# Loading the FFN weights early and in chunks in a fused attention and FFN kernel on eight cores

## The chip, the cores and the metric

The kernel runs on one Trainium2 chip, on all of its 8 cores. Each core computes its own 2 of the 16 sequences with the same program; nothing is exchanged between cores. The metric is the device time of one execution in microseconds, that of the slowest core.

## What is computed

One layer: windowed attention over channels, residual and layer norm, then a gated FFN with int weights scaled by 1/127, residual and layer norm. Cut to what matters:

```python
# x: (16, 4096, 1024) f32; W_qkv (1024, 3072); W_out (1024, 1024)
# w_gate, w_up: (3072, 1024) int32; w_down: (1024, 3072) int32
def attn(x, W_qkv, b_qkv, W_out, b_out):      # 16 heads of 64, windows of 256, step 128
    qkv = (x @ W_qkv + b_qkv)                  # q, k, v per head
    a = einsum('bhndw,bhnew->bhnde', qw, kw) * 64 ** -0.5
    o = einsum('bhnde,bhnew->bhndw', softmax(a), vw)
    return o.reshape(...)[:, :L] @ W_out + b_out
def ffn(x, w_gate, w_up, w_down):
    gate = einsum('bsd,hd->bsh', x, w_gate / 127)
    up = einsum('bsd,hd->bsh', x, w_up / 127)
    return einsum('bsh,dh->bsd', silu(gate) * up, w_down / 127)
x = layernorm(x + attn(x, ...))
out = layernorm(x + ffn(x, ...))
```

## The kernel before

The program has two phases, each an instruction block of its own, written with one queue of instructions per engine and explicit semaphore waits. SP and POOL issue all DMAs: SP the plain loads, POOL the stores and the loads that cast f32 or int32 to bf16.

**Phase A** is attention. For each of the core's 2 sequences it walks over t = 0 to 17: step t makes q, k and v for one block of 128 rows (three passes of matmuls, L498 and L503, against `wqkv_bf`, which holds all of W_qkv in SBUF: 128 partitions x 8 x 3072 bf16, 48 KB each), the scores of window t-1, and for window t-2 the transposes, the second attention matmul, the copies `attn_out` (L751, ScalarE), the output projection (L697, L702), the residual `y1pre` (L720, VectorE) and the layer norm (L769 to L804, ScalarE). One window's output is 256 rows, handled as two halves k2. Each half needs its rows of x again, in f32, in `xr32`: SP loads them at L685, 512 KB each, two buffers, each load waiting for the residual two halves before. The last qkv pass belongs to t = 16 of the second sequence; the windows 14 and 15 (steps t = 16 and 17) are finished after it. The results go to DRAM twice, as `y1dbg` in f32 (L731, POOL) and, transposed and in bf16, as `y1fm_scr` (L345, POOL). The next window's attention waits for the residual of the one before (L631).

In between, phase A prepares the FFN weights: 56 jobs (24 for gate, 24 for up, 8 for down), each a casting load into `w_in_bf`, a scaling on VectorE (L389), transposes on TensorE (L403), a copy to `wT_stage` (L413) and a store to a scratch tensor in DRAM (L423 and L426: `wgT_scr`, `wuT_scr`, `wdT_scr`). Two jobs run in a step; the last job is left over and runs after the last step. Its stores stand behind the `y1dbg` stores in POOL's queue.

**Phase B** is the FFN. All engines first wait for everything of phase A (`a_end`), since its SBUF tiles lie where those of phase A did. Then SP loads the three transposed weights whole, 6144 KB each, with one DMA each on one semaphore, `wl0` (L921 to L923), and each matmul group of the gate waits for all three (`wload_tok`). The loop runs over 32 groups g of 256 rows. SP's loads for group g are 8 of `y1fm_sb` (64 KB each, L942) and 2 of `y1r32` (512 KB each, L950), two buffers each. In a group, 24 steps hc go over the hidden units, 128 at a time: 8 matmuls for gate (L984, 128x256 results), 8 for up (L993), SiLU on ScalarE (L1071), the product `h_bf` on VectorE (L1014), and, one step behind, 4 matmuls for down (L965, L969). TensorE's order in a step is gate(hc), up(hc), down(hc-1). Then come the residual `y2pre` (L1034) and the second layer norm, whose work is spread over the steps of the next group.

Of the kernel before, what the change touches and what calls it, by code (L numbers as in the profile page):

```python
# [9 lines left out]
BF16 = mybir.dt.bfloat16  # L10
# [50 lines left out]
def build_program(debug=False, seqs=SEQS, l=L):  # L61
# [32 lines left out]
    for s in ["T", "V", "A", "G",  # L94
              "xq0", "xq1", "xq2", "xq3", "xr0", "xr1", "wl0",
              "tx0", "tx1", "tv0", "tv1", "ty0", "ty1", "tw0", "tw1",
              "wc0", "wc1", "wc2", "wc3", "wi0", "pk0", "pk1", "pf0", "pf1", "pw0", "pw1",
              "yf0", "yf1", "yr0", "yr1", "st0", "st1"]:
        b.sem(s)
# [11 lines left out]

    wqkv_bf = SA("wqkv_bf", [128, 8, 3 * D], BF16)
    wout_bf = SA("wout_bf", [128, 8, D], BF16)
# [130 lines left out]
    with nc.Block() as blk:  # L244
# [212 lines left out]
        def prep_trs(n_tr):  # L457
            k = 0
            while wprep_tr[0] < wprep_ld[0] and k < n_tr:
# [4 lines left out]
                k += 1  # L464

        emit_xload(0)
        emit_xload(1)
# [4 lines left out]
        for s in range(SEQSv):  # L472
            for t in range(TB + 1):
# [113 lines left out]
                if have_qkv:  # L587
                    emit_qkv_pass(2)
                    qkv_free[0] = evac_half[((gt, 2), 1)]
                    emit_xtr(gt + 2)  # L590

                if have_qkv:
# [247 lines left out]
        while wprep_tr[0] < len(wprep_jobs):  # L840
# [4 lines left out]
            wprep_tr[0] += 1  # L845
        flush_typf()

        @blk.sync
# [15 lines left out]
    SBB = lambda n, sh, dt, **kw: es_b.enter_context(nc.sbuf_tensor(n, sh, dt, **kw))  # L864
    wgT = SBB("wgT", [128, 24, D], BF16)
    wuT = SBB("wuT", [128, 24, D], BF16)
# [29 lines left out]
    with nc.Block() as blk:  # L896
# [20 lines left out]
        @blk.sync  # L917
        def _(q):
            for tk in a_end:
                b.wait(q, "Q", tk)  # L920
            b.inc(q.dma_start(wgT[:, :, :], wgT_h.ap().transpose([1, 0, 2])), "wl0", 16)  # L921
            b.inc(q.dma_start(wuT[:, :, :], wuT_h.ap().transpose([1, 0, 2])), "wl0", 16)  # L922
            b.inc(q.dma_start(wdT[:, :, :], wdT_h.ap().transpose([1, 0, 2])), "wl0", 16)  # L923
        wload_tok = b.tok("wl0")

        b2bases = {}

        def nb2(g):
            return b2bases[g] + (24 if g == 0 else 40)

        for g in range(NGg):
            s = g // (Lv // 256)
            r0 = 256 * (g % (Lv // 256))
            gsl = g % 2
            b2base = [b.cnt["A"] if g == 0 else nb2(g - 1)]
            b2bases[g] = b2base[0]

# [15 lines left out]
            rload_done[g] = b.tok("yr%d" % gsl)  # L953

            def emit_down(hc, g=g):
                hsl = hc % 2

                @blk.tensor
                def _(t_, g=g, hc=hc, hsl=hsl):
                    b.wait(t_, "T", mul_done[(g, hc)])  # L960
                    if hc == 0:
# [13 lines left out]
            for hc in range(24):  # L975
# [3 lines left out]
                def _(t_, g=g, gsl=gsl, hc=hc, hsl=hsl):  # L979
                    b.wait(t_, "T", wload_tok)  # L980
                    b.wait(t_, "T", dload_done[g])
# [7 lines left out]
                @blk.tensor  # L989
                def _(t_, g=g, gsl=gsl, hc=hc, hsl=hsl):  # L990
                    b.wait(t_, "T", mul_done.get((g, hc - 2) if hc >= 2 else (g - 1, 22 + hc)))
                    for dc in range(8):
                        b.inc(t_.matmul(up_ps[hsl], wuT[:, hc, 128 * dc:128 * (dc + 1)],  # L993
                                        y1fm_sb[:, gsl, dc, :],
                                        start=(dc == 0), stop=(dc == 7)), "T", 1)
# [27 lines left out]
                if hc >= 1:  # L1023
                    emit_down(hc - 1)
            emit_down(23)

# [11 lines left out]
            for rs in range(2):  # L1038
                apply2_done[(g, rs)] = ("A", nb2(g) + (8 + 8 * rs if g == NGg - 1 else 26 + 3 * rs))

            def emit_vln2(rs, g=g, s=s, r0=r0):
# [136 lines left out]
```

How the kernel before makes its waits and increments, by code:

```python
    def inc(self, instr, name, by=1):  # L40
        instr.then_inc(self.sems[name], by)
        self.cnt[name] += by
        return (name, self.cnt[name])
# [4 lines left out]
    def wait(self, eng, engkey, tok):  # L48
        if tok is None:
            return
        name, val = tok
        if val <= 0:
            return
        key = (engkey, name)
        if self.waited.get(key, 0) >= val:
            return
        self.waited[key] = val
        eng.wait_ge(self.sems[name], val)
# [1085 lines left out]
        @blk.gpsimd  # L1144
        def _(g_):
            g_.wait_ge(b.sems["st0"], b.cnt["st0"])
            g_.wait_ge(b.sems["st1"], b.cnt["st1"])
```

## Time and profile before

| what | us |
|---|---|
| median of 3 executions | 3465.74 (3463.91 to 3727.74) |
| the profiled execution | 3468.05 |
| its span on the slowest core (core 5) | 3466.5 |
| spans of the eight cores | 3447.6 to 3466.5 |
| TensorE busy | 2970.2 (86%) |
| last matmul of phase A to first of phase B | 82.4 |

A page of the profile is one execution on the slowest core. Its parts are the busy time of each engine, the span in slices, the DMA queues, the chain of work that ended last, the costliest groups of instructions, and the DMA issues with their size and the time from issue to landing. PE is TensorE, PEld its weight loads, DVE VectorE, ACT ScalarE, POOL GpSimd, SP SyncE; L12 is a line of the kernel. The granted clock is the share of full speed that TensorE's clock was given in a stretch. Behind the page the trace can be asked for any stretch: the timeline of instructions, the waits by who waited for whom, and tables of busy time by window.

### The profile page before, as it was taken

How to read it: one execution, taken by the hardware profiler on the slowest of the kernel's cores; microseconds unless marked ns; L12 is line 12 of the kernel's file. 1: busy time of each engine (PE TensorE's matmuls, PEld its weight loads, DVE VectorE, ACT ScalarE, POOL GpSimd, SP SyncE). 2: the span in 40 equal slices, each digit the busy share in tenths (PEclk: the TensorE clock that was granted, in tenths of full speed). 3: DMA queues.
4: the chain of work that ended last, by engine and by line, in shares of the span. 5: the costliest groups of instructions: out<-in, count | busy, mean ns of one | idle time of the engine just before them, and what ended most of it. 6: DMA issues, size and time to landing. Idle time of an engine off the chain costs nothing.

```text
span 3466.5 us, 61589 instructions; the slowest of 8 cores (3447.6 to 3466.5 us)
## 1 busy us (share of the span) xinstructions
PE 2970.2 (86%) x23572; PEld 1996.9 (58%) x23572; DVE 935.4 (27%) x1750; ACT 1248.6 (36%) x2721; POOL 184.1 (5%) x324
## 2 busy tenths in 40 slices
PE   1877787778766772599999999999999999999997
PEld 0344444344433331377777777777777777777775
DVE  0434444344433331022122122221222222212211
ACT  0245454524443343034334233343332333433323
POOL 1001111101111100000000000000000000000000
PEclk9999999899998896799999999999999999999998
DMA  7134434333443324511111011111110111111100
GB/s 128 49 88 125 110 107 119 101 86 98 122 128 103 104 80 155 169 39 42 44 50 44 32 50 44 45 36 44 50 44 31 50 44 50 36 39 50 44 32 25
DMA packets 108737, 245.73 MB, mean 71 GB/s; under 512 B 11424, under 2 KB 44192, under 8 KB 108448
## 3 DMA queue, kind: packets, MB, share of 16 engines
q0 software_dynamic: 43744, 138.96, 14.1%
q1 hardware_dynamic: 64704, 102.82, 8.9%
q8 instruction: 193, 3.16, 0.4%
q14 instruction: 96, 0.79, 0.1%
HBM read 175.16 MB, written 102.76 MB: 80 GB/s over the span
## 4 chain that ended last, share of the span: by engine, by line
PE 58%; SPq 2%; ACT 0%; DMA 0%; DVE 0%; issue 0%; POOL 0%; ACTq 0%; DVEq 0%; POOLq 0%
PE psum_qkv L984 19%; PE psum_O L965 10%; PE psum_S L993 10%; PE psum_TR L993 10%; PE psum_O L969 10%; SPq L942 1%; SPq L923 1%; SPq L922 0%; DMA y1fm_sb<-y1fm_scr 0%; DVE y2pre L1034 0%; ACT y L1141 0%; ACT y2sq L1124 0%; ACT y2sq L1121 0%; ACT L1121 0%; DVE h_bf L1014 0%
## 5 line engine op out<-in xcount | busy, mean ns | idle before, releaser
L984 PE MATMUL psum_qkv<-y1fm_sb,wgT 128*128 128x256 bf16 x6144 | 797.9, 273 | 82.4 <-DMA y1fm_sb<-y1fm_scr 82.4
L984 PEld LDWEIGHTS psum_qkv<-y1fm_sb,wgT 128*128 128x128 bf16 x6144 | 601.8, 98 | 309.8 <-issue 82.7
L1071 ACT ACTIVATE sg_bf<-psum_qkv 128x256 bf16<-128x256 f32 x768 | 293.7, 382 | 1181.6 <-PE psum_S L993 672.6
L965 PE MATMUL psum_O<-wdT,h_bf 128*128 128x512 bf16 x1536 | 581.9, 379 | 0.6 <-DVE h_bf L1014 0.6
L969 PE MATMUL psum_O<-wdT,h_bf 128*128 128x512 bf16 x1536 | 582.0, 379 | 0.0
L993 PE MATMUL psum_S<-y1fm_sb,wuT 128*128 128x256 bf16 x3072 | 399.0, 273 | 0.0
L993 PE MATMUL psum_TR<-y1fm_sb,wuT 128*128 128x256 bf16 x3072 | 398.6, 273 | 0.0
L1014 DVE TENSOR_TENSOR h_bf<-psum_S,sg_bf 128x256 bf16<-128x256 f32 x384 | 163.1, 425 | 815.6 <-PE psum_O L965 717.4
L1014 DVE TENSOR_TENSOR h_bf<-psum_TR,sg_bf 128x256 bf16<-128x256 f32 x384 | 163.1, 425 | 795.0 <-PE psum_O L965 675.7
L498 PE MATMUL psum_qkv<-wqkv_bf,x_fm 128*128 128x512 bf16 x816 | 315.3, 386 | 48.8 <-DVE q_tm L531 44.3
L993 PEld LDWEIGHTS psum_S<-y1fm_sb,wuT 128*128 128x128 bf16 x3072 | 301.0, 98 | 35.2
L993 PEld LDWEIGHTS psum_TR<-y1fm_sb,wuT 128*128 128x128 bf16 x3072 | 300.9, 98 | 35.1
L503 PE MATMUL psum_qkv<-wqkv_bf,x_fm 128*128 128x512 bf16 x816 | 314.5, 385 | 7.6 <-DVE q_tm L534 7.1
L697 PE MATMUL psum_O<-wout_bf,attn_out 128*128 128x512 bf16 x512 | 228.1, 446 | 8.4 <-ACT attn_out L751 8.4
L702 PE MATMUL psum_O<-wout_bf,attn_out 128*128 128x512 bf16 x512 | 224.3, 438 | 0.4 <-ACT attn_out L751 0.4
L965 PEld LDWEIGHTS psum_O<-wdT,h_bf 128*128 128x128 bf16 x1536 | 150.0, 98 | 119.9 <-issue 21.2
L969 PEld LDWEIGHTS psum_O<-wdT,h_bf 128*128 128x128 bf16 x1536 | 150.0, 98 | 98.6
L769 ACT ACTIVATE y1sq<-y1pre 128x1024 f32<-128x1024 f32 x64 | 67.6, 1057 | 300.3 <-DVE y1pre L720 297.1
L498 PEld LDWEIGHTS psum_qkv<-wqkv_bf,x_fm 128*128 128x128 bf16 x816 | 80.7, 99 | 154.8 <-issue 72.9
L1071 ACT ACT_TABLE_LOAD x63 | 80.8, 1283 | 193.2 <-PE psum_S L993 98.5
L751 ACT ACT_TABLE_LOAD x32 | 41.1, 1283 | 298.7 <-PE psum_S L311 160.7
L1058 POOL DMA_DIRECT2D out<-y x64 | 34.1, 533 | 2074.0 <-ACT y L1105 1860.1
(145 smaller groups left out, 2441.9 us busy)
## 6 DMA issues: line engine op xcount, KB each, us to landing
xr<-x SPq DMA_DIRECT2D x64, 512.0 KB, 3.2
y1dbg<-y_f POOLq DMA_DIRECT2D x64, 512.0 KB, 3.0
y1r<-y1dbg SPq DMA_DIRECT2D x64, 512.0 KB, 4.2
out<-y POOLq DMA_DIRECT2D x64, 512.0 KB, 2.9
y1fm_scr<-y1fm_stage POOLq DMA_DIRECT2D x8, 2048.0 KB, 7.2
y1fm_sb<-y1fm_scr SPq DMA_DIRECT2D x256, 64.0 KB, 2.0
xt_bf<-x POOLq DMA_DIRECT2D x34, 256.0 KB, 8.1
wqkv_bf<-wqkv POOLq DMA_DIRECT2D x8, 768.0 KB, 27.9
```

What stands on the lines that cost most here:

```text
L498: b.inc(t_.matmul(psum_qkv[:, 0:512], lhsT, wqkv_bf[:, c, 1024 * p:1024 * p + 512], start=(c == 0), stop=False), "T", 1)
L503: b.inc(t_.matmul(psum_qkv[:, 512:1024], lhsT, wqkv_bf[:, c, 1024 * p + 512:1024 * (p + 1)], start=(c == 0), stop=False), "T", 1)
L697: b.inc(t_.matmul(pj[:, 0:512], lhsT, wout_bf[:, c, 0:512], start=(c == 0), stop=False, skip_group_check=True), "T", 1)
L702: b.inc(t_.matmul(pj[:, 512:1024], lhsT, wout_bf[:, c, 512:1024], start=(c == 0), stop=False, skip_group_check=True), "T", 1)
L751: b.inc(a.activation(attn_out[:, hp, rb:rb + 256] .rearrange("p (d c) -> p d c", c=4), psum_O[:, base:base + 256] .rearrange("p (c d) -> p ...
L769: b.inc(a.activation(y1sq[:, :], y1pre[:, rsl, :], AF.Identity, accum_out=sums[:, rsl, :]), "A", 1)
L965: b.inc(t_.matmul(down_ps[:, 1024 * rs:1024 * rs + 512], lhsT, wdT[:, hc, 0:512], start=(hc == 0), stop=(hc == 23), skip_group_check=True) ...
L969: b.inc(t_.matmul(down_ps[:, 1024 * rs + 512:1024 * (rs + 1)], lhsT, wdT[:, hc, 512:1024], start=(hc == 0), stop=(hc == 23), skip_group_ch ...
L984: b.inc(t_.matmul(gate_ps[hsl], wgT[:, hc, 128 * dc:128 * (dc + 1)], y1fm_sb[:, gsl, dc, :], start=(dc == 0), stop=(dc == 7)), "T", 1)
L993: b.inc(t_.matmul(up_ps[hsl], wuT[:, hc, 128 * dc:128 * (dc + 1)], y1fm_sb[:, gsl, dc, :], start=(dc == 0), stop=(dc == 7)), "T", 1)
L1014: b.inc(v.tensor_tensor(h_bf[:, hsl, :], up_ps[hsl], sg_bf[:, hsl, :], ALU.mult), "V", 1)
L1071: b.inc(a.activation(sg_bf[:, hsl, :], gate_ps[hsl], AF.Silu), "A", 1)
```

## The change

- `wqkv_bf` is placed at the other end of SBUF (`side="right"`) in a stack of its own, which is closed after the last qkv pass has been emitted; `wgT`, of the same size, is then opened in its place.
- `emit_wg_stream`, called in the last qkv step of the last sequence (t = 16), right after the last qkv pass, puts into SP's queue: a wait for the last qkv matmul, waits for the stores of the prepared weights emitted so far, and the load of `wgT`, 6144 KB in one DMA, with its own semaphore `wg0`. It stands ahead of the `xr32` loads of window 14 in SP's queue.
- In phase B the three big loads are gone. `emit_gloads` holds the loads of a group; those of g = 0 and 1 stand first in SP's queue, those of g + 2 follow after group g.
- `wuT` and `wdT` are loaded in 24 chunks each of 128 x 1024 bf16 (256 KB). Up front come wu 0, wd 0, wu 1, wd 1, wd 2; in group 0, after step hc, chunk hc + 2 of each. wu(hc) waits for up(hc - 2), wd(hc) for down(hc - 3), with semaphores taken in turn (two for wu, three for wd).
- TensorE waits for `wg_tok` before a gate group, for `wu_tok[hc]` before up and `wd_tok[hc]` before down.

```diff
@@ -92,7 +92,8 @@
     es_outer = contextlib.ExitStack()
     b = Bld(nc, es_outer)
     for s in ["T", "V", "A", "G",
-              "xq0", "xq1", "xq2", "xq3", "xr0", "xr1", "wl0",
+              "xq0", "xq1", "xq2", "xq3", "xr0", "xr1",
+              "wl0", "wl1", "wl2", "wl3", "wl4", "wg0",
               "tx0", "tx1", "tv0", "tv1", "ty0", "ty1", "tw0", "tw1",
               "wc0", "wc1", "wc2", "wc3", "wi0", "pk0", "pk1", "pf0", "pf1", "pw0", "pw1",
               "yf0", "yf1", "yr0", "yr1", "st0", "st1"]:
@@ -109,7 +110,10 @@
     es_a = contextlib.ExitStack()
     SA = lambda n, sh, dt, **kw: es_a.enter_context(nc.sbuf_tensor(n, sh, dt, **kw))
 
-    wqkv_bf = SA("wqkv_bf", [128, 8, 3 * D], BF16)
+    es_qkv = contextlib.ExitStack()
+    wqkv_bf = es_qkv.enter_context(
+        nc.sbuf_tensor("wqkv_bf", [128, 8, 3 * D], BF16, side="right"))
+    wgT_holder = [None]
     wout_bf = SA("wout_bf", [128, 8, D], BF16)
     bq_rep = SA("bq_rep", [128, 3 * D], BF16)
     bo_rep = SA("bo_rep", [128, D], BF16)
@@ -463,6 +467,20 @@
                 wprep_tr[0] += 1
                 k += 1
 
+        def emit_wg_stream(gt_last):
+            es_qkv.close()
+            wgT_holder[0] = es_outer.enter_context(
+                nc.sbuf_tensor("wgT", [128, 24, D], BF16, side="right"))
+            pw_fin = [b.tok("pw0"), b.tok("pw1")]
+
+            @blk.sync
+            def _(q, gt_last=gt_last, pw_fin=pw_fin):
+                b.wait(q, "Q", qkv_mm_done[(gt_last, 2)])
+                for tk in pw_fin:
+                    b.wait(q, "Q", tk)
+                b.inc(q.dma_start(wgT_holder[0][:, :, :],
+                                  wgT_h.ap().transpose([1, 0, 2])), "wg0", 16)
+
         emit_xload(0)
         emit_xload(1)
         emit_xload(2)
@@ -588,6 +606,9 @@
                     emit_qkv_pass(2)
                     qkv_free[0] = evac_half[((gt, 2), 1)]
                     emit_xtr(gt + 2)
+
+                if s == SEQSv - 1 and t == TB - 1 and wprep_tr[0] >= 24:
+                    emit_wg_stream(gt)
 
                 if have_qkv:
                     vbk, vqtok = claim_tr()
@@ -844,6 +865,9 @@
             prep_transpose(wprep_tr[0])
             wprep_tr[0] += 1
         flush_typf()
+        if wgT_holder[0] is None:
+            emit_wg_stream(SEQSv * TB - 1)
+        wg_tok = b.tok("wg0")
 
         @blk.sync
         def _(q):
@@ -862,7 +886,7 @@
 
     es_b = contextlib.ExitStack()
     SBB = lambda n, sh, dt, **kw: es_b.enter_context(nc.sbuf_tensor(n, sh, dt, **kw))
-    wgT = SBB("wgT", [128, 24, D], BF16)
+    wgT = wgT_holder[0]
     wuT = SBB("wuT", [128, 24, D], BF16)
     wdT = SBB("wdT", [128, 24, D], BF16)
     y1fm_sb = SBB("y1fm_sb", [128, 2, 8, 256], BF16)
@@ -918,22 +942,29 @@
         def _(q):
             for tk in a_end:
                 b.wait(q, "Q", tk)
-            b.inc(q.dma_start(wgT[:, :, :], wgT_h.ap().transpose([1, 0, 2])), "wl0", 16)
-            b.inc(q.dma_start(wuT[:, :, :], wuT_h.ap().transpose([1, 0, 2])), "wl0", 16)
-            b.inc(q.dma_start(wdT[:, :, :], wdT_h.ap().transpose([1, 0, 2])), "wl0", 16)
-        wload_tok = b.tok("wl0")
-
-        b2bases = {}
-
-        def nb2(g):
-            return b2bases[g] + (24 if g == 0 else 40)
-
-        for g in range(NGg):
+
+        wu_tok, wd_tok = {}, {}
+
+        def emit_wu_chunk(hc):
+            @blk.sync
+            def _(q, hc=hc):
+                b.wait(q, "Q", up_done.get((0, hc - 2)))
+                b.inc(q.dma_start(wuT[:, hc, :], wuT_h.ap()[hc]),
+                      "wl%d" % (hc % 2), 16)
+            wu_tok[hc] = b.tok("wl%d" % (hc % 2))
+
+        def emit_wd_chunk(hc):
+            @blk.sync
+            def _(q, hc=hc):
+                b.wait(q, "Q", down_done.get((0, hc - 3)))
+                b.inc(q.dma_start(wdT[:, hc, :], wdT_h.ap()[hc]),
+                      "wl%d" % (2 + hc % 3), 16)
+            wd_tok[hc] = b.tok("wl%d" % (2 + hc % 3))
+
+        def emit_gloads(g):
             s = g // (Lv // 256)
             r0 = 256 * (g % (Lv // 256))
             gsl = g % 2
-            b2base = [b.cnt["A"] if g == 0 else nb2(g - 1)]
-            b2bases[g] = b2base[0]
 
             @blk.sync
             def _(q, g=g, s=s, r0=r0, gsl=gsl):
@@ -952,11 +983,32 @@
                           "yr%d" % gsl, 16)
             rload_done[g] = b.tok("yr%d" % gsl)
 
+        emit_gloads(0)
+        if NGg > 1:
+            emit_gloads(1)
+        for c0 in (0, 1):
+            emit_wu_chunk(c0)
+            emit_wd_chunk(c0)
+        emit_wd_chunk(2)
+
+        b2bases = {}
+
+        def nb2(g):
+            return b2bases[g] + (24 if g == 0 else 40)
+
+        for g in range(NGg):
+            s = g // (Lv // 256)
+            r0 = 256 * (g % (Lv // 256))
+            gsl = g % 2
+            b2base = [b.cnt["A"] if g == 0 else nb2(g - 1)]
+            b2bases[g] = b2base[0]
+
             def emit_down(hc, g=g):
                 hsl = hc % 2
 
                 @blk.tensor
                 def _(t_, g=g, hc=hc, hsl=hsl):
+                    b.wait(t_, "T", wd_tok[hc])
                     b.wait(t_, "T", mul_done[(g, hc)])
                     if hc == 0:
                         b.wait(t_, "T", resid2_done.get((g - 1, 1)))
@@ -977,7 +1029,7 @@
 
                 @blk.tensor
                 def _(t_, g=g, gsl=gsl, hc=hc, hsl=hsl):
-                    b.wait(t_, "T", wload_tok)
+                    b.wait(t_, "T", wg_tok)
                     b.wait(t_, "T", dload_done[g])
                     b.wait(t_, "T", silu_done.get((g, hc - 2) if hc >= 2 else (g - 1, 22 + hc)))
                     for dc in range(8):
@@ -988,6 +1040,7 @@
 
                 @blk.tensor
                 def _(t_, g=g, gsl=gsl, hc=hc, hsl=hsl):
+                    b.wait(t_, "T", wu_tok[hc])
                     b.wait(t_, "T", mul_done.get((g, hc - 2) if hc >= 2 else (g - 1, 22 + hc)))
                     for dc in range(8):
                         b.inc(t_.matmul(up_ps[hsl], wuT[:, hc, 128 * dc:128 * (dc + 1)],
@@ -1022,6 +1075,10 @@
                     pending_vln2[0] = None
                 if hc >= 1:
                     emit_down(hc - 1)
+                if g == 0 and hc + 2 <= 23:
+                    emit_wu_chunk(hc + 2)
+                    if hc >= 1:
+                        emit_wd_chunk(hc + 2)
             emit_down(23)
 
             for rs in range(2):
@@ -1037,6 +1094,9 @@
 
             for rs in range(2):
                 apply2_done[(g, rs)] = ("A", nb2(g) + (8 + 8 * rs if g == NGg - 1 else 26 + 3 * rs))
+
+            if g + 2 < NGg:
+                emit_gloads(g + 2)
 
             def emit_vln2(rs, g=g, s=s, r0=r0):
                 rstd2_done = ("A", nb2(g) + (7 + 8 * rs if g == NGg - 1 else 22 + rs))
```

## Rows read from the trace of the kernel before

**Rows 1.** The page's first lines, and the waits of all engines: waited for, times, longest.

```profile
span 3466.5 us, 61589 instructions; the slowest of 8 cores (3447.6 to 3466.5 us)
PE 2970.2 (86%) x23572; PEld 1996.9 (58%) x23572; DVE 935.4 (27%) x1750; ACT 1248.6 (36%) x2721; POOL 184.1 (5%) x324
...
PE psum_qkv L984 <- DMA y1fm_sb<-y1fm_scr: 82.4, 1, 82.4
```

**Rows 2.** Timeline (start, duration, engine, line) of TensorE, 1338 to 1460 us.

```profile
1343.28 1.01 PE L311 MATMUL psum_qkv<-ident_sb,y_bf 128*128 128x128 bf16 x8 [10.93 <-DVE wT_stage L413]
...
1426.74 1.86 PE L984 MATMUL psum_qkv<-y1fm_sb,wgT 128*128 128x256 bf16 x8 [82.45 <-DMA y1fm_sb<-y1fm_scr]
...
1428.39 1.91 PE L993 MATMUL psum_S<-y1fm_sb,wuT 128*128 128x256 bf16 x8
...
1430.10 1.91 PE L984 MATMUL psum_qkv<-y1fm_sb,wgT 128*128 128x256 bf16 x8
...
1433.99 1.04 PE L984 MATMUL psum_qkv<-y1fm_sb,wgT 128*128 128x256 bf16 x8
...
1434.86 1.04 PE L993 MATMUL psum_S<-y1fm_sb,wuT 128*128 128x256 bf16 x8
...
1436.60 1.04 PE L984 MATMUL psum_qkv<-y1fm_sb,wgT 128*128 128x256 bf16 x8
```

**Rows 3.** Timeline of SP, 1359 to 1430 us; the duration is that of the issues.

```profile
1359.32 0.38 SPq L921 DMA_DIRECT2D wgT<-wgT_scr  x1
1359.75 13.65 SPq L922 DMA_DIRECT2D wuT<-wuT_scr  x1
1373.45 20.88 SPq L923 DMA_DIRECT2D wdT<-wdT_scr  x1
1394.37 26.77 SPq L942 DMA_DIRECT2D y1fm_sb<-y1fm_scr  x8
...
1422.12 4.12 SPq L942 DMA_DIRECT2D y1fm_sb<-y1fm_scr  x8
```

**Rows 4.** Timeline of DVE and POOL at the end of phase A.

```profile
1298.40 1.23 DVE L720 TENSOR_TENSOR y1pre<-psum_O,xr 128x1024 f32<-128x1024 f32 x1 [7.49 <-PE psum_O L697]
...
1338.38 0.53 POOL L731 DMA_DIRECT2D y1dbg<-y_f  x1 [6.95 <-ACT y_f L801]
...
1349.51 0.89 POOL L345 DMA_DIRECT2D y1fm_scr<-y1fm_stage  x1 [0.74 <-issue]
```

**Rows 5.** Table by windows: length, busy us, then granted clock, DMA share, GB/s.

```profile
1290.00:1310.00 20.00, 11.78 (x60) 5.49 (x60) 6.52 (x10) 13.01 (x30) 0.53 (x1) 0.82 0.22 79
...
1375.00:1395.00 20.00, 0.00 (x0) 0.00 (x0) 0.00 (x0) 0.00 (x0) 0.00 (x0) 0.50 0.98 303
...
1427.00:1447.00 20.00, 20.00 (x136) 14.46 (x135) 2.97 (x7) 3.97 (x8) 0.00 (x0) 0.86 0.18 64
```

**Rows 6.** DMA issues over the span: count, KB each, median us to landing.

```profile
xr<-x SPq DMA_DIRECT2D x64, 512.0 KB, 3.2
...
y1fm_sb<-y1fm_scr SPq DMA_DIRECT2D x256, 64.0 KB, 2.0
...
wgT<-wgT_scr SPq DMA_DIRECT2D x1, 6144.0 KB, 25.0
```

**Rows 7.** L942 in two windows: landing of the first and second set of 8.

```profile
L942 SPq DMA_DIRECT2D y1fm_sb<-y1fm_scr x8: 477/600/19652, 1394.4 to 1420.5; - x8
...
DMA to landing us min/median/max: 4.2/6.7/26.7
...
DMA to landing us min/median/max: 2.8/3.7/5.0
```

**Rows 8.** Timeline of SP and TensorE; L423's stores between 1000 and 1300 us.

```profile
1265.75 0.33 SPq L685 DMA_DIRECT2D xr<-x  x1
...
1282.85 0.38 PE L510 MATMUL psum_qkv<-bq_rep,ones 128*128 128x512 bf16 x1
...
L423 POOL DMA_DIRECT2D wdT_scr<-wT_stage x21: 885/885/927, 1032.0 to 1198.9; - x21
```

## The prediction

> **What bounds the kernel now.** I read the page first. TensorE is busy 86% of a span of 3466.5 us, and most of the list of waits is engines waiting for TensorE; the one wait of TensorE itself that stands out is 82.4 us, once, on the loads of y1fm_sb [rows 1]. Then I read the timeline of that spot. TensorE ends its last transposes of phase A at 1344.3 (1343.28 + 1.01) and starts the first gate group of phase B at 1426.74 [rows 2]. SP issues its first DMA of phase B at 1359.32 [rows 3]; before that it waits for the last store of y1fm_scr, which POOL issued at 1349.51 [rows 4]. So the hole has two parts: 15.0 us of storing (1359.3 - 1344.3) and 67.4 us in which 3 x 6144 KB of weights and then y1fm_sb come in (1426.7 - 1359.3). The table by windows shows that second part as DMA at 0.98 of its time and 303 GB/s with no matmul [rows 5]. The rest of phase B is TensorE back to back: a step over one hidden chunk (8 gate, 8 up, 4 down matmuls) is 1436.60 - 1433.99 = 2.61 us, its gate group 0.87 us [rows 2], and there the change alters nothing.
>
> **The sum goes against** the profiled execution's own 3468.05 us; the median of the runs is 3465.74, 2.3 us less.
>
> **Phase B, what goes.** TensorE no longer waits for the three big loads. In SP's queue now come the group loads of g=0 (8 of y1fm_sb, 2 of y1r32), those of g=1, and then wu0, wd0, wu1, wd1, wd2. Call T0 the moment of SP's first DMA (1359.3 before). An issue takes 0.43 us and 0.04 us to the next: the second set of 8 took 4.12 us in all with one long one in it [rows 3], and I give the y1r32 loads the same. The 8 loads of g=0 are out at T0 + 3.8; they land 2.0 us after issue when nothing is ahead [rows 6], so gate 0 starts near T0 + 5.5. That is not yet the gain: up 0 needs wu0, and wu0 is the 21st DMA. 20 issues x 0.47 = 9.4 us. What it then takes to land: the trace has no 256 KB load here, the nearest rows are 2.0 us for 64 KB and 3.2 for 512 KB on an idle queue [rows 6], which would be about 2.5, and 2.8 to 5.0, median 3.7, for the second set of y1fm_sb, which had 1 MB of y1r32 ahead [rows 7]. wu0 stands in the second position (3 MB issued ahead of it in 9.4 us, about what 303 GB/s [rows 5] carries), so I take 3.7 and keep 2.5 and 5.0. Up 0 then starts at T0 + 9.4 + 3.7 + 0.1 = T0 + 13.2. wd0, wu1, wd1 and wd2 follow 0.47 us apart and are wanted 3 us later or more at the clock of that moment (gate 1 alone takes 1.7, below).
>
> **Phase B, the stream.** Chunk hc+2 of wu is issued once up(hc) is done and wanted at up(hc+2). Between lie down(hc-1), gate(hc+1), up(hc+1), down(hc) and gate(hc+2), five blocks of 0.87 us: 4.35 us of cover. It needs about 0.1 for the semaphores and 2.5 to land (2.0 and 3.2 as bounds). So 1 to 2 us are to spare and it costs nothing; wd has one step more. Both are issued on SP, where only each other's waits are in the way: wd(hc+2) waits for down(hc-1), 0.87 us after up(hc). The load is 0.52 MB in 2.61 us = 201 GB/s, under the 303 of [rows 5]. If a chunk landed in 5.0 us, the worst of the loaded rows [rows 7], each of 22 steps would lose 0.7 us, 15 in all: the upper bound. SP's own next work, the loads of g=2, comes behind the last chunk, and is wanted only a group (over 60 us) later as before. [...]
>
> **Phase A, what is added.** The load of wgT (6144 KB) goes into SP's queue ahead of the xr32 loads of window 14 of the second sequence. Before, the first of those was issued at 1265.75 [rows 8], right after the y1pre of the window before, and was wanted by the y1pre at 1298.40 [rows 4]. Now SP first waits for the last qkv matmul, which starts at 1282.85 and ends at 1283.2 (the weight stores it also waits for are long out: the 21 of wdT_scr before 1300 begin by 1198.9, and the last job's three are emitted behind) [rows 8], and issues wgT at 1283.3. The next DMA on the queue is not through until half of the big one is gone: wuT behind wgT took 13.65 us to issue, wdT behind wuT 20.88, and y1fm_sb's first 19.65 of the 26.77 that its eight took [rows 3]. So xr32's issue ends at 1283.8 + 13.7 = 1297.5, just when it is wanted. Its data stand behind the rest of wgT, which lands 25.0 us after its issue [rows 6], at 1308.4, and 0.5 MB more at 303 GB/s is 1.7 us: 1310.1, and y1pre at 1310.2 instead of 1298.4. That is a delay of d = 11.8 us.
>
> Would it be absorbed? Layer norm of both halves goes straight into the attn_out copies, proj and LN of window 15; ACT and TensorE alternate to y_f, y1dbg at 1338.38, the wdT_scr store queued behind it on POOL, and y1fm_scr at 1349.51 [rows 4]. Each waits for the one ahead, so all d reaches the end of phase A, and T0 becomes 1371.1. The bounds of d: the first y1fm_sb read as landed 26.7 us after issue start [rows 7], that is 1421.1, or 7.1 after its issue ended; by that xr32 lands at 1304.6 and d = 6.2. Above: a slower landing under the other cores' load, 13. The first y1fm_sb shares its semaphore with seven others, so I trust the full landing more and take 11.8.
> The Trainium skill, page "DMA: Bandwidth & Descriptors", section "Queues, rings and completion order", says that each DMA engine takes the descriptors of a ring in order and that all rows of one issuing engine share those rings. By it xr32 can't overtake wgT and the sum is the one with 11.8; by the early reading of the row it would be 5.6 us better. The trace leaves it open.
>
> **The clock.** After the hole TensorE's granted clock is at its lower level (1.2 GHz): the up group takes 1.71 us start to start, and 0.87 at full clock (2.4 GHz) a few us later [rows 2]; the window from 1427 to 1447 has 0.86 [rows 5]. The same ramp is paid after the change, but gate 0 is cut off from up 0 by 5 us of waiting, so perhaps one group more runs slow: 1.0 us (0 to 3).
>
> **Sum.** Up 0 starts at 1371.1 + 13.2 = 1384.3 instead of 1428.39 [rows 2]: -44.1. The clock: +1.0. Stream: 0. That is 3468.05 - 43.1 = 3425.0 for the profiled execution, and less 2.3 it is 3423 for the median.
>
> **Rivals.**
> *A, the xr32 loads lose nothing* (d = 0: wgT is spread so that the later DMA gets through, or xr32 lands in time). For it speaks only the early landing of [rows 7]. The gain is 55, time 3411.
> *B, the stream stalls lightly.* Landings of 4.6 to 5.5 us; for it speak the 5.0 of [rows 7], against it that those had other loads ahead. 0.3 to 1.2 us x 22 = 7 to 26 us: 3430 to 3449.
> *C, slower than before: the stream stalls and TensorE stays at half clock through g=0.* In the attention tail, where TensorE works in bursts between waits, the granted clock is 0.82 [rows 5]. If each of 24 steps ran at half clock, each would cost 2.61 more, less some 2 us of ramp already paid: +60, and 3423 + 60 = 3483, 17 slower than before. At half clock the cover is 8.7 us too, so the stall would have to be long: it decides from about 6.4 us per landing (4.35 + 44/22), which no row of a 64 or 512 KB load on SP beside normal traffic shows [rows 6].
> The Trainium skill, page "TensorE: Matmul & The Clock Gate", section "HAM oscillation — how this bites in real kernels", describes just this: a loop whose tiles each wait for a DMA runs with the array held at half clock. It speaks against the change only if there is a wait in each step; by it the time is C's.
> *D, more in the attention tail.* The hole of 12 us there drops the clock once more, or xr32's second load comes late too: 5 to 10 us, 3428 to 3433. Against it: the tail was already mostly slow or waiting.
>
> **Chances.** Forecast 0.70 (alone 3413 to 3432), A 0.08, B 0.12, C 0.04, D 0.06. The range 3406 to 3440 holds the forecast, A, D and the lower half of B. Two per cent, about what a measurement can tell from no change, is 69.3 us. More than the 67.4 us that lie between T0 and the first matmul can't be had, and the g=0 loads must still come; so faster by over 2% gets 0.02, slower by over 2% (C with heavy stalls besides) 0.02, within 2% 0.96.
>
> **What would show it.** In the profile after: (1) TensorE's longest wait on y1fm_sb falls from 82.4 to some 20 us, with a second one of about 5 us on wuT; (2) the xr32 load of window 14 shows an issue of some 13 us and y1pre at about 1310; (3) SP's first DMA of phase B near 1371; (4) the first gate near 1377, up 0 near 1384; (5) the 24 steps of g=0 in about 65 us at a clock of 0.9 or more. The forecast is wrong if y1pre stays at 1298 (A), if up matmuls in g=0 wait for wuT in every step (B), or with a clock below 0.8 there (C).

## The result and the profile after

The changed kernel is faster by 1.2%: the ratio to the kernel before is 0.9883, 95% interval 0.9869 to 0.9897, which makes 3425 us of 3466. That is clear of noise, and under two per cent. Executions in which a die ran at a lowered clock are left out of it. The forecast was 3423 with a range of 3406 to 3440. The profiled execution took 3430.02 us against 3468.05, 38 us less, where 43.1 less had been forecast for it.

The page's first lines, and the waits of TensorE from 1200 to 1460 us on the slowest core, which is core 6 here (waited for, in total, times, longest):

```profile
span 3428.5 us, 61374 instructions; the slowest of 8 cores (3411.3 to 3428.5 us)
PE 2937.0 (86%) x23218; PEld 1995.8 (58%) x23572; DVE 935.6 (27%) x1750; ACT 1247.8 (36%) x2721; POOL 184.1 (5%) x324
...
PE psum_qkv L1036 <- DMA y1fm_sb<-y1fm_scr: 22.1, 1, 22.1
PE psum_qkv L315 <- ACT y_bf L825: 17.0, 1, 17.0
PE psum_qkv L315 <- DVE wT_stage L417: 10.9, 1, 10.9
...
PE psum_S L1046 <- DMA wuT<-wuT_scr: 7.9, 1, 7.9
```

The wait of 82.4 us [rows 1] has become 22.1, and two smaller ones stand beside it: 7.9 us on the first chunk of wuT, and in the attention tail a wait for y_bf, which was 5.3 us before and is 17.0. The timelines of SP, DVE and TensorE show where each comes from (some lines of each):

```profile
1285.60 0.39 SPq L481 DMA_DIRECT2D wgT<-wgT_scr  x1
1286.08 29.16 SPq L706 DMA_DIRECT2D xr<-x  x4
1373.02 3.81 SPq L973 DMA_DIRECT2D y1fm_sb<-y1fm_scr  x8
1376.88 0.92 SPq L981 DMA_DIRECT2D y1r<-y1dbg  x2
1377.83 4.79 SPq L973 DMA_DIRECT2D y1fm_sb<-y1fm_scr  x8
1382.67 0.91 SPq L981 DMA_DIRECT2D y1r<-y1dbg  x2
1383.62 0.43 SPq L952 DMA_DIRECT2D wuT<-wuT_scr  x1
```

```profile
1312.29 2.55 DVE L741 TENSOR_TENSOR y1pre<-psum_O,xr 128x1024 f32<-128x1024 f32 x2 [19.18 <-DMA xr<-x]
```

```profile
1381.19 1.87 PE L1036 MATMUL psum_qkv<-y1fm_sb,wgT 128*128 128x256 bf16 x8 [22.11 <-DMA y1fm_sb<-y1fm_scr]
1391.00 1.86 PE L1046 MATMUL psum_S<-y1fm_sb,wuT 128*128 128x256 bf16 x8 [7.94 <-DMA wuT<-wuT_scr]
1392.66 1.67 PE L1036 MATMUL psum_qkv<-y1fm_sb,wgT 128*128 128x256 bf16 x8
1394.17 1.04 PE L1046 MATMUL psum_TR<-y1fm_sb,wuT 128*128 128x256 bf16 x8
```

y1pre now waits 19.18 us for xr32, where it used to wait 7.49 for the projection [rows 4]. Phase B's first DMA goes out at 1373.02 instead of 1359.32, and up 0 starts at 1391.00 instead of 1428.39 [rows 2, 3]. After that the stream costs nothing to see: a step of group 0 takes 2.61 us, as before. In the table by windows (core 6; the last three columns are granted clock, DMA share and GB/s), TensorE is busy throughout while 201 GB/s come in:

```profile
1400.00:1420.00 20.00, 19.84 (x151) 14.86 (x153) 3.40 (x8) 2.77 (x8) 0.00 (x0) 1.00 0.62 201
```

The cores differ by more than some of the terms: on the same core the last qkv matmul can come 10 us sooner or later from execution to execution. So the stages below are measured from events inside each core, as the mean of all eight, taken from the timelines of each (y1pre is the residual of the window's first half). "Tail" runs from the start of the last qkv matmul to SP's first DMA of phase B (T0), "head" from T0 to up 0, "group 0" from up 0 to the first y2pre. All in us.

| kernel | last qkv to y1pre of window 14 | tail | head | group 0 |
|---|---|---|---|---|
| before | 15.34 | 75.77 | 67.25 | 63.39 |
| changed | 25.05 | 85.59 | 16.78 | 64.11 |
| difference | +9.7 | +9.8 | -50.5 | +0.7 |

Together -40.0 us; the ratio gives -40.6. Within a microsecond the whole effect is in these three stages.

### The profile page after: what moved, and what is told of

It is laid out like the page before. It is cut to its first block, busy times and chain, and to the rows that moved or that the text cites. A ratio compares the mean times of both kernels' runs of the same rounds, so it can differ in the third digit from the quotient of the medians.

```text
span 3428.5 us, 61374 instructions; the slowest of 8 cores (3411.3 to 3428.5 us)
## 1 busy us (share of the span) xinstructions
PE 2937.0 (86%) x23218; PEld 1995.8 (58%) x23572; DVE 935.6 (27%) x1750; ACT 1247.8 (36%) x2721; POOL 184.1 (5%) x324
## 4 chain that ended last, share of the span: by engine, by line
PE 58%; issue 1%; ACT 0%; SPq 0%; DMA 0%; DVE 0%; POOL 0%; ACTq 0%; DVEq 0%; POOLq 0%
PE psum_qkv L1036 20%; PE psum_O L1021 11%; PE psum_S L1046 10%; PE psum_TR L1046 10%; PE psum_O L1017 8%; SPq L973 0%; DMA wuT<-wuT_scr 0%; DVE y2pre L1091 0%; ACT y L1201 0%; ACT y2sq L1184 0%; ACT y2sq L1181 0%; SPq L981 0%; ACT L1181 0%; DVE h_bf L1067 0%; ACT l2ln L1197 0%
## 5 line engine op out<-in xcount | busy, mean ns | idle before, releaser
L1036 PE MATMUL psum_qkv<-y1fm_sb,wgT 128*128 128x256 bf16 x6144 | 797.7, 273 | 22.1 <-DMA y1fm_sb<-y1fm_scr 22.1
L1021 PE MATMUL psum_O<-wdT,h_bf 128*128 128x512 bf16 x1536 | 582.0, 379 | 18.6 <-issue 5.7
L1017 PE MATMUL psum_O<-wdT,h_bf 128*128 128x512 bf16 x1280 | 484.9, 379 | 0.0
L516 PE MATMUL psum_qkv<-wqkv_bf,x_fm 128*128 128x512 bf16 x754 | 290.7, 385 | 47.5 <-DVE q_tm L549 42.7
L521 PE MATMUL psum_qkv<-wqkv_bf,x_fm 128*128 128x512 bf16 x814 | 313.5, 385 | 15.0 <-DVE q_tm L552 7.1
L1046 PEld LDWEIGHTS psum_TR<-y1fm_sb,wuT 128*128 128x128 bf16 x3072 | 300.6, 98 | 34.8
L723 PE MATMUL psum_O<-wout_bf,attn_out 128*128 128x512 bf16 x512 | 225.0, 439 | 16.8 <-ACT attn_out L772 11.0
L718 PE MATMUL psum_O<-wout_bf,attn_out 128*128 128x512 bf16 x480 | 209.1, 436 | 0.0
L516 PEld LDWEIGHTS psum_qkv<-wqkv_bf,x_fm 128*128 128x128 bf16 x816 | 80.6, 99 | 153.3 <-issue 70.8
L521 PEld LDWEIGHTS psum_qkv<-wqkv_bf,x_fm 128*128 128x128 bf16 x816 | 80.8, 99 | 109.0 <-issue 23.9
```

Of the source, the lines that this page charges most:

```text
L516: b.inc(t_.matmul(psum_qkv[:, 0:512], lhsT, wqkv_bf[:, c, 1024 * p:1024 * p + 512], start=(c == 0), stop=False), "T", 1)
L521: b.inc(t_.matmul(psum_qkv[:, 512:1024], lhsT, wqkv_bf[:, c, 1024 * p + 512:1024 * (p + 1)], start=(c == 0), stop=False), "T", 1)
L718: b.inc(t_.matmul(pj[:, 0:512], lhsT, wout_bf[:, c, 0:512], start=(c == 0), stop=False, skip_group_check=True), "T", 1)
L723: b.inc(t_.matmul(pj[:, 512:1024], lhsT, wout_bf[:, c, 512:1024], start=(c == 0), stop=False, skip_group_check=True), "T", 1)
L1017: b.inc(t_.matmul(down_ps[:, 1024 * rs:1024 * rs + 512], lhsT, wdT[:, hc, 0:512], start=(hc == 0), stop=(hc == 23), skip_group_check=True) ...
L1021: b.inc(t_.matmul(down_ps[:, 1024 * rs + 512:1024 * (rs + 1)], lhsT, wdT[:, hc, 512:1024], start=(hc == 0), stop=(hc == 23), skip_group_ch ...
```

## The experiments

The lengths of stages are read from the profiled execution of each kernel; ratios, always to the kernel before on the same chip, come from the timed executions and are given where there were enough.

### wgT behind window 14's loads of x

```diff
-                if s == SEQSv - 1 and t == TB - 1 and wprep_tr[0] >= 24:
-                    emit_wg_stream(gt)
...
+                    if s == SEQSv - 1 and t == TB - 1 and wprep_tr[0] >= 24:
+                        emit_wg_stream(gt)
```

The call moves from behind the last qkv pass to behind both halves of window 14, and SP's wait for the last qkv matmul moves with it.

> The load of wgT stands behind the two xr32 loads of window 14 in SP's queue instead of ahead of them; nothing else. Theory (the tail is late because the xr32 load stands behind wgT in one queue): y1pre of window 14 starts 15.5 us after the last qkv matmul as before, not 25; the xr32 load of window 15 is issued some 16 us after wgT and lands by 10 us after y1pre's neighbour, 12 us before it is wanted; T0 comes 9.8 us earlier, the time is 3415 us, 10 under the changed kernel. Rival (the tail is late because wgT's transfer takes bandwidth from everything, or the loss only moves to window 15): 3422 to 3427 us.

y1pre starts 15.55 us after the last qkv matmul on every core, and the tail is 75.5 us: as before, to 0.3. The head stays at 17.2. SP's timeline (core 0) shows two loads of x before wgT and the next two 16 us behind it, early enough for window 15:

```profile
1263.90 4.21 SPq L703 DMA_DIRECT2D xr<-x  x2
1281.56 0.38 SPq L481 DMA_DIRECT2D wgT<-wgT_scr  x1
1297.84 4.21 SPq L703 DMA_DIRECT2D xr<-x  x2
1356.26 3.71 SPq L973 DMA_DIRECT2D y1fm_sb<-y1fm_scr  x8
```

The ratio is 0.9857 (0.9829 to 0.9884). It agrees with 10 us less, but executions of the kernel before scattered from 3467 to 3483 us on this chip, so the stage is the better witness. The 10 us of the tail come from the place in SP's queue of this one DMA with its waits.

### wgT from POOL's queue

This tells apart three reasons that the trial above leaves together: the queue, the bandwidth, and SP's wait for the last qkv matmul, which stays where it was.

```diff
             def _(q, gt_last=gt_last, pw_fin=pw_fin):
                 b.wait(q, "Q", qkv_mm_done[(gt_last, 2)])
                 for tk in pw_fin:
                     b.wait(q, "Q", tk)
+
+            @blk.gpsimd
+            def _(q, gt_last=gt_last, pw_fin=pw_fin):
+                b.wait(q, "G", qkv_mm_done[(gt_last, 2)])
+                for tk in pw_fin:
+                    b.wait(q, "G", tk)
                 b.inc(q.dma_start(wgT_holder[0][:, :, :],
```

> The load of wgT is issued by POOL at the same moment, on POOL's queue; SP keeps its wait for the last qkv matmul at the same place, so the xr32 loads of window 14 are issued when wgT is. Theory (xr32 was late because its data stood behind wgT's in one queue): xr32 lands within 8 us of its issue, y1pre of window 14 starts 15.5 us after the last qkv matmul as before, T0 75.5 us after it. Rival (the transfer of 6 MB takes the bandwidth whatever the queue): xr32 lands 12 us or more after its issue, y1pre 17 to 25 us after the last qkv matmul. Rival (SP's wait alone made it late): y1pre at 25 us as in the changed kernel.

y1pre comes 15.33 to 15.56 us after the last qkv matmul on all eight cores; the tail is 75.5 us. Core 4: SP issues the first two loads of x at 1276.2 and 1276.6, POOL wgT at 1276.6, and the four loads of x around it land in 6.2 us (median) beside the 6 MB transfer, against the 3.2 that is the median over the kernel before [rows 6], while wgT takes 28.0. From the line of xr32 (issue times and landing), and from the DMA issues of 1275 to 1320 us:

```profile
L712 SPq DMA_DIRECT2D xr<-x x4: 327/328/488, 1276.2 to 1296.3; - x4
...
DMA to landing us min/median/max: 4.1/6.2/8.1
...
wgT<-wgT_scr POOLq DMA_DIRECT2D x1, 6144.0 KB, 28.0
```

The first two loads go out just ahead of wgT, so they alone would not tell its queue from its place in time. The next two do: on core 4 they are issued 16 and 20 us behind wgT and land at 1300.6 and 1303.5, before its 1304.6, and the first of them lands 2.2 to 4.9 us before wgT on every core. In the trial above, on one queue, the same load landed 1.2 to 1.3 us after wgT on every core.

So on core 4 the shared bandwidth costs a 512 KB load 3 us at the median and 5 at most, and on the slowest core, 0, 7 (10.1 us to land), which the 15 us of lead hide on all cores; a shared queue costs the whole transfer ahead. SP's wait costs nothing: it stood at its place here, and so it does in the next trial.

### Streaming alone

```diff
-                b.inc(q.dma_start(wgT_holder[0][:, :, :],
-                                  wgT_h.ap().transpose([1, 0, 2])), "wg0", 16)
...
+        @blk.sync
+        def _(q):
+            b.inc(q.dma_start(wgT[:, :, :], wgT_h.ap().transpose([1, 0, 2])), "wg0", 16)
...
```

The load stands in phase B, ahead of the loads of group 0; SP's waits of `emit_wg_stream` stay where they were.

> wgT is loaded whole at the head of phase B, behind a_end, ahead of the loads of group 0; the chunks of wu and wd stream as in the changed kernel. Theory (two separate terms: the early load costs about 10 us in the attention tail and the streaming saves time in phase B): the tail is as in the kernel before (last qkv matmul to SP's first DMA of phase B 75.8 us, mean of the cores), and up 0 starts some 21 us later after that DMA than in the changed kernel, 16.8 + 21 = 38 us, instead of 67.2 before. Gain over the kernel before 29 us, 3437 us. Rival (the streaming alone brings the whole gain, the early load only moves wgT's time about): up 0 at 17 to 25 us, gain over 40 us, below 3426. Rival (the stream stalls behind a big load): every up group in group 0 waits, gain under 15 us.

The tail is 75.80 us as before, the head 34.86 (38 expected): 32.4 us of the head's 67.25 are gone. The theory holds, and the rival that gave the streaming the whole gain (up 0 at 17 to 25 us) falls. The big load costs the head 18 us, a little less than the 21 taken for it. SP's timeline (core 0, where the last qkv matmul starts at 1281.73) has the loads of x right behind SP's wait, and y1pre comes 15.55 us after that matmul on every core:

```profile
1282.35 20.44 SPq L704 DMA_DIRECT2D xr<-x  x4
1357.71 0.38 SPq L984 DMA_DIRECT2D wgT<-wgT_scr  x1
```

### The early load alone

```diff
-        for c0 in (0, 1):
-            emit_wu_chunk(c0)
-            emit_wd_chunk(c0)
-        emit_wd_chunk(2)
+
+        @blk.sync
+        def _(q):
+            b.inc(q.dma_start(wuT[:, :, :], wuT_h.ap().transpose([1, 0, 2])), "wl0", 16)
+            b.inc(q.dma_start(wdT[:, :, :], wdT_h.ap().transpose([1, 0, 2])), "wl1", 16)
...
```

> Only the first half of the change: wgT early as in the changed kernel, wu and wd whole, one DMA each, behind the loads of groups 0 and 1. Theory (the gain is in what TensorE need not wait for, and most of it is the streaming): up 0 some 30 us after SP's first DMA of phase B, the first down group 52 to 54 us after it, against 67.2 for up 0 and some 72 for the first down before; less the 10 us of the tail that leaves 6 to 10 us under the kernel before. Rival (moving a third of the bytes away brings a third of the gain and more, 20 us): down at 40 us or sooner.

The tail is 85.73, the head 36.68, group 0 81.03 with its second wait in it. Head and group 0 together make 117.7 instead of 130.6; less the 10 us of the tail, 3 us remain. That is less than the 6 to 10 expected, since wu took 37 us from T0 to be there and not 30, and the first down group started at T0 + 56.3 (mean) and not 52 to 54. One execution was timed, so there is no ratio to set beside the 3 us. The waits of TensorE (core 2):

```profile
PE psum_S L1050 <- DMA wuT<-wuT_scr: 28.9, 1, 28.9
PE psum_qkv L1040 <- DMA y1fm_sb<-y1fm_scr: 21.8, 1, 21.8
PE psum_qkv L315 <- ACT y_bf L825: 15.6, 1, 15.6
PE psum_O L1021 <- DMA wdT<-wdT_scr: 14.1, 1, 14.1
```

The early load by itself brings little: TensorE's next group needs the other 12 MB. Only with the streaming, which takes the other two from the path, does it bring 18 us in the head (34.86 to 16.78) for 10 lost in the tail.

### The stream with less cover

```diff
-                b.wait(q, "Q", up_done.get((0, hc - 2)))
+                b.wait(q, "Q", up_done.get((0, hc - 1)))
                 b.inc(q.dma_start(wuT[:, hc, :], wuT_h.ap()[hc]),
...
```

Chunk hc + 1 of wu is asked for after step hc, and of wu only chunk 0 still stands up front; wd is as it was.

> Chunk hc of wu is asked for after up(hc-1) instead of up(hc-2); TensorE then has 1.74 us of other work before it wants it, and the chunks land 2.8 us after issue. Theory (the stream was free because its cover of 4.35 us is over the landing time, and the clock stands short waits): a wait of about 1.2 us in each of 22 steps, the clock at its upper level, 26 us more than the changed kernel, 3451 us. Rival C of the prediction (a wait on a DMA in every step holds the clock at half): steps of 5.2 us instead of 2.6, granted clock near 0.5 over group 0, some 60 us more, 3480 to 3485 us. Rival (the cover plays no part): within 5 us of the changed kernel.

Group 0 takes 95.16 us, 31.1 more than in the changed kernel (26 expected). On core 4 TensorE waits 34.8 us for wuT in 24 waits; without the first, of 7.5, that is 27.3, or 1.19 each. On the mean of the cores the waits behind the first make 26.8 us; the other 4 us of the 31.1 are not in waits for wuT, and what they are is left open. The timeline and the windows of core 4:

```profile
1423.62 1.04 PE L1035 MATMUL psum_qkv<-y1fm_sb,wgT 128*128 128x256 bf16 x8
1426.15 1.03 PE L1045 MATMUL psum_TR<-y1fm_sb,wuT 128*128 128x256 bf16 x8 [1.50 <-DMA wuT<-wuT_scr]
...
1427.88 1.04 PE L1035 MATMUL psum_qkv<-y1fm_sb,wgT 128*128 128x256 bf16 x8
1429.90 1.03 PE L1045 MATMUL psum_S<-y1fm_sb,wuT 128*128 128x256 bf16 x8 [0.98 <-DMA wuT<-wuT_scr]
```

```profile
1420.00:1440.00 20.00, 14.05 (x104) 9.60 (x103) 2.12 (x5) 1.92 (x5) 0.00 (x0) 1.00 0.45 134
1440.00:1460.00 20.00, 14.21 (x105) 9.66 (x103) 2.13 (x5) 1.92 (x5) 0.00 (x0) 1.00 0.47 138
```

A wait of 1.2 us in every step leaves the granted clock at 1.00, its upper level of 2.4 GHz, with TensorE busy 70% of the time. From 8 us behind up 0 to the end of group 0 it is 1.00 on five cores and 0.98 to 0.99 on the other three. The rival that held the clock at half falls for waits of this length; longer ones were not tried. The cover is shown to be what makes the stream free: cover less landing is what is paid or spared. This kernel's span also grew on cores 6 and 7 later in phase B, which the stage does not hold; nothing is concluded from its total time.

### The first chunks ahead of the other loads

```diff
-        emit_gloads(0)
-        if NGg > 1:
-            emit_gloads(1)
+        emit_yload(0, range(8))
         for c0 in (0, 1):
             emit_wu_chunk(c0)
             emit_wd_chunk(c0)
         emit_wd_chunk(2)
...
+                    if 6 <= hc < 14:
+                        emit_yload(1, [hc - 6])
+                    if hc == 21:
+                        emit_rload(0)
+                        emit_rload(1)
```

`emit_gloads` is split in two: `emit_yload` loads y1fm_sb (a list of its eight parts) and `emit_rload` y1r32.

> In phase B the chunks wu0, wd0, wu1, wd1, wd2 stand right behind the 8 loads of y1fm_sb for group 0; y1fm_sb for group 1 comes one DMA a step in steps 6 to 13, the y1r32 loads of groups 0 and 1 behind the last chunk. Theory (up 0 is late by what stands ahead of wu0 in SP's queue, 12 more issues and 2.5 MB): wu0 is issued at T0 + 3.8 and lands 3 us later, up 0 at T0 + 7 instead of T0 + 16.8, time 3415 to 3417 us. Rival (up 0 is bound by what a first chunk takes to land anyway): up 0 at T0 + 12 or later, 3421 us or more. Rival (the moved loads stall the end of group 0): a wait of y2pre on y1r32, gain under 5 us.

The head is 7.64 us instead of 16.78: 9.1 less, as the theory has it; wu0 is issued at T0 + 3.8 and lands in 3.0 us (means). Group 0 reads 66.2 here, but on cores 4, 6 and 7 it is 63.6 to 64.2, with a granted clock of 0.98 or more, and on the others of this execution up to 69.3, where the clock reads 0.91. On this chip it also reads 65.2 without the edit (the trial with wgT behind the loads of x), and with the edit on another chip (below) it is 64.5. So the moved loads cost group 0 at most about 1 us. The ratio is 0.9883 (0.9846 to 0.9921), too wide to show 9 us. TensorE's waits around group 0 (core 1) no longer name wuT.

### Both edits

wgT behind window 14's loads of x, and the first chunks first: the two diffs above together, run twice, the second time beside the changed kernel.

> The edits of both trials together: wgT behind window 14's xr32 loads, and the first chunks ahead of the other loads in phase B. Theory (the two terms are separate and add): SP's first DMA 75.5 us after the last qkv matmul, up 0 at 7.6 us after that, 50.5 + 9.3 = 60 us under the kernel before, ratio 0.983. Rival (what one edit gives the other takes back, since the chunks then meet other traffic): ratio 0.985 or more.

> The kernel with both edits once more, beside the changed kernel on one chip. Theory (the terms add: 10 us in the attention tail and 9 us at the head of phase B): 19 us under the changed kernel, 60 under the kernel before, ratio 0.983. Rival (only one of the two reaches the end): 10 us under the changed kernel.

> The changed kernel as it is, beside the one with both edits. Both theories: ratio 0.988 as measured.

| kernel | last qkv to y1pre | tail | head | ratio (95% interval) |
|---|---|---|---|---|
| both, first time | 15.55 | 75.56 | 7.71 | 0.9852 (0.9817 to 0.9888) |
| both, again | 14.92 | 75.31 | 7.35 | 0.9825 (0.9812 to 0.9838) |
| changed kernel, again | 24.55 | 85.10 | 16.59 | 0.9883 (0.9868 to 0.9898) |

The last two ran on one chip. There both edits together are 0.58% under the changed kernel, about 20 us of 3468, where the stages say 9.8 + 9.2 = 19.0. The terms add, and the two intervals do not overlap. The ratio of the first time, 0.9852, would by itself have fitted the rival as well; its interval is too wide to decide. The start of phase B in the second profiled execution (SP, then TensorE, core 6):

```profile
1358.16 3.65 SPq L973 DMA_DIRECT2D y1fm_sb<-y1fm_scr  x8
1361.85 0.43 SPq L952 DMA_DIRECT2D wuT<-wuT_scr  x1
```

```profile
1363.49 1.87 PE L1043 MATMUL psum_qkv<-y1fm_sb,wgT 128*128 128x256 bf16 x8 [19.87 <-DMA y1fm_sb<-y1fm_scr]
1365.15 1.91 PE L1053 MATMUL psum_S<-y1fm_sb,wuT 128*128 128x256 bf16 x8
```

Up 0 follows gate 0 without a wait.

### The hole's other part: two attempts

What remains is the time from the last transposes to T0. First, both edits and the leftover weight job done in its turn, in step 14:

```diff
-                if wprep_tr[0] + 2 > wprep_ld[0]:
+                if (wprep_tr[0] + 2 > wprep_ld[0]
+                        and wprep_ld[0] < len(wprep_jobs)):
                     break
```

> As the trial with both edits, and the last job of the weight preparation, which was left over to the end of phase A, is transposed in its turn at step t = 14 of the second sequence. Theory (the end of phase A waits for three stores of that job one after the other on POOL, between y1dbg and y1fm_scr): SP's first DMA of phase B comes about 9 us sooner after the last qkv matmul, 66 to 67 us instead of 75.5, for 1 to 2 us more in the step that takes the job; ratio 0.981. Rival (those stores lie beside the layer norm of the last half, or the job costs the step as much): within 3 us of the trial with both.

The tail falls from 75.6 to 67.9 us (67.3 to 68.4 on the eight cores), near what was expected, but the last qkv matmul comes 13.7 us later (1290.2 instead of 1276.5, mean of the cores; 1276.4 to 1280.4 in the other kernels). The ratio is 0.9853 (0.983 to 0.9876), no better. The rival holds: the job costs the steps at least as much as it costs the end.

Second, both edits and the last store of y1fm_scr cut, so that only window 15's 512 KB are left for the end:

```diff
-                    if (n0 % 4 == 3) or (n0 == NW - 1):
+                    if n0 == NW - 2:
+                        emit_pf(gw0, s0, n0)
+                    elif n0 == NW - 1:
+                        emit_pf(gw0, s0, n0, 3)
+                    elif n0 % 4 == 3:
                         emit_pf(gw0, s0, n0)
...
```

The fourth argument of `emit_pf` is the first of the four windows in the stage that the store takes.

> Both edits, and the last store of y1fm_scr of each sequence cut in two: windows 12 to 14 are stored when 14 is done, so that the store behind which phase B waits is 512 KB instead of 2048. Theory (the hole's first part is the landing time of that store, 9.4 us for 2 MB): it lands in 3 to 4 us, SP's first DMA of phase B comes 5 to 6 us sooner, 70 us after the last qkv matmul; ratio 0.9815. Rival (the wait is for something else, or the landing is fixed cost): within 2 us of the kernel with both edits.

The tail is 71.68 us against 75.31 in the kernel with both edits: 3.6 less, not 5 to 6. The last issue on POOL and SP's wait for it (core 2):

```profile
1352.33 0.89 POOL L349 DMA_DIRECT2D y1fm_scr<-y1fm_stage  x1
...
SPq L58 <- DMA y1fm_scr<-y1fm_stage: 11.2, 1, 11.2
```

SP's wait was 15.1 us on this core in the kernel with both edits. The store itself lands in 3.4 to 3.7 us on the eight cores, where it took 7.1 to 7.7, and that is the whole 3.6: the mechanism was right. The 9.4 us taken for the old landing is about the time from that store's issue to SP's first DMA (8.7 to 9.3), and the 1.6 or 1.7 us from the landing to that DMA stay with the smaller store. The ratio, 0.9823 (0.9808 to 0.9837), can't be told from 0.9825. So the stage shows a gain of 3.6 us and the total can't confirm it.

## Why the prediction was right, and where its terms were off

The path was right: every one of the waits that the prediction named is there in the profile after, and what it said of their causes is borne out by the trials. Two of its terms were mis-sized, one in the head and one in the tail.

**The head.** That TensorE would wait for wu0 and not for y1fm_sb was right, and the queue ahead of wu0 was its cause (the trial with the chunks first). Its size was off: T0 + 13.2 was forecast and the mean is 16.8. The term mis-sized is wu0's landing: 3.7 us were taken from [rows 7], and 5.9 to 7.3 were measured, mean 6.7. The issue came at T0 + 10.0 (mean) and not 9.4, too. The row it took had 1 MB ahead of it, wu0 had 3. The check by bandwidth hid this: that 303 GB/s carries about 3 MB in 9.4 us supposes that the queue runs at this rate from its first issue, and it does not. The loads of 64 KB go out one in 0.47 us, which is 139 GB/s at most, and the windows of core 6 show it: 98 and 160 GB/s in the first two stretches of 4 us behind T0, then 266, and 351 only from T0 + 12 on, when 2.1 MB of 3.4 are in. On the other cores the first stretch has 44 to 105 GB/s and the second 179 to 299, so the slow start is common to all. The pace of the issues accounts for the first stretch; why the second is slower on some cores than on others is not shown.

```profile
1373.00:1377.00 4.00, 0.00 (x0) 0.00 (x0) 0.00 (x0) 0.00 (x0) 0.00 (x0) 0.50 0.35 98
1377.00:1381.00 4.00, 0.00 (x0) 0.00 (x0) 0.00 (x0) 0.00 (x0) 0.00 (x0) 0.50 0.59 160
...
1385.00:1391.00 6.00, 0.00 (x0) 0.03 (x1) 0.00 (x0) 0.00 (x0) 0.00 (x0) 0.50 0.99 351
```

**The tail.** Queue order, not bandwidth nor the wait, was the cause: shown by two trials. All of the delay reached the end: +9.7 at y1pre, +9.8 at T0. The forecast was 11.8. The mis-sized term is wgT's landing: the 25.0 us of [rows 6] are those of core 5, the slowest of the eight in the kernel before, where the mean is 23.4 (21.6 to 25.0), and 20.8 to 25.3 were measured in the changed kernel, mean 23.0. xr32 landed 1.2 us after wgT on core 6 (1286.08 + 26.0 against 1285.60 + 25.3), where 1.7 was taken, and 1.2 to 1.4 on the others. The issue of xr32 was held for 10.6 to 14.5 us, but it was over 11.6 to 15.5 us after the last qkv matmul, no later than y1pre wanted the data (15.5), so most of the delay is the landing behind wgT and not the hold. The early landing read from the first y1fm_sb in [rows 7] was rightly not believed: in no core did xr32 land ahead of wgT.

**The stream** cost nothing, with the chunks landing in 2.8 us (wu) and 3.1 (wd) at the median of core 6, 2.5 forecast, under a cover of 4.35. The two more waits in a step cost nothing either: 2.61 us a step before and after. The slowest chunk of wu in the stream took 4.5 us (core 5), and TensorE waited 0.4 us for it, once. With 1.74 of cover the stream costs what is short.

**The clock.** +1.0 us forecast, +0.7 measured as the longer group 0.

The errors partly cancel. Against -43.1 stand +3.6 in the head, -2.0 in the tail and -0.3 in the clock, and +1.8 since the sum was made on core 5, whose head before was 69.1 and not the mean of 67.3: -40.0, what the stages show. That 3425 lay so near to 3423 is in part luck: the head came 3.6 us late and the tail 2.0 early. Of the rivals, A (no loss in the tail) did not happen but is what the reordered kernel reaches; B (light stalls) did not, though the slowest landing, 4.5 us, was past the cover; C did not, the granted clock being 1.00 from 1400 to 1440 us on every core, and in the trial of less cover waits of 1.2 us in every step did not bring it on either; D did not, since of the 9.8 us at T0 9.7 stood at y1pre already.

The Trainium skill, page "DMA: Bandwidth & Descriptors", section "Queues, rings and completion order", which the prediction weighed, says that each DMA engine takes the descriptors of a ring in order: the trace agrees, xr32 lands 1.2 us after wgT on one queue and 6.2 us after its own issue (median of core 4), with wgT still under way, on two. Its sibling section "Issuing engines are not separate DMA queues" says that issuing from several engines only saves the sequencer's time. The measurement goes against the "only": with wgT issued by POOL the tail is 10 us shorter than with wgT on SP's queue ahead of the loads of x, and there the loads of x that are issued behind wgT land before it.

The page "TensorE: Matmul & The Clock Gate" of the Trainium skill, section "HAM oscillation — how this bites in real kernels", tells of a loop held at half clock by a DMA wait in every tile. Its case has waits of about 3 to 5 us, longer than the matmuls between them, and the prediction, which called it "just this", took it for waits of any length. In the trial with less cover the loop waits too, 1.2 us in a step of about 4, and the granted clock stays at 1.00, so C's half clock does not follow from a short wait in each step. No run here has a loop with waits as long as the page's.

## What to carry to other kernels

Before a big prefetch is put into a DMA queue, look at what is queued behind it and when that is wanted: one 6 MB load ahead of a 512 KB load cost 10 of the 18 us that loading early had won, and moving it behind that load gave them back. In a stream of chunks count the cover in work between asking and wanting (here 4.35 us against 2.8 to land), and put the first chunk ahead of everything that is not needed before it. Moving one of three loads off a path on which all three are needed at once brings little (3 us here); it pays once the others are streamed.

## What was not expected of the hardware

- A 512 KB load issued right behind a 6 MB one on the same queue is itself held at issue for 10.6 to 14.5 us and lands 1.2 to 1.4 us after the big one. With the big one on another queue, loads issued 16 us behind it still land before it, and a load takes 4.1 to 8.1 us (core 4), where 3.2 is the median of the kernel before.
- TensorE keeps the upper clock with a wait of 1.2 us (mean of core 4) in every step of about 4 us, busy 70%.
- After 3 MB of loads in 10 us, a chunk of 256 KB takes 5.9 to 7.3 us to land and not the 2.8 of the steady stream; on core 6 the DMA engines move 98, 160, 266 and then 351 GB/s in the stretches from T0 on.
